# A cross-attention block on one core: VectorE scales the fourth head, ScalarE makes the second high part of K and Q ahead of that head's exponentials, x's statistics spread over four places

## The reference

```python
h = _layernorm(x, gamma, beta)                       # x: (8, 256, 256)
Q = (h @ Wq).reshape(B, NQ, 16, 64)                  # Wq: (256, 1024)
K = (context @ Wk).reshape(B, NC, 16, 64)            # context: (8, 256, 192)
V = (context @ Wv).reshape(B, NC, 16, 64)
attn = jnp.einsum('bihd,bjhd->bhij', Q, K)
attn = jax.nn.softmax(attn, axis=-1) * 64 ** -0.5
vals = jnp.einsum('bhij,bjhd->bihd', attn, V).reshape(B, NQ, 1024)
return x + vals @ Wo + bo
```

## Time and profile before

| | |
|---|---|
| time, median of 3 runs | 335.07 us (335.03 to 335.29) |
| the profiled execution's own time | 335.13 us |
| its span in the profile | 333.3 us |
| TensorE (PE) busy | 323.3 us, 97% |
| ScalarE (ACT) busy | 254.8 us, 76% |
| VectorE (DVE) busy | 234.6 us, 70% |
| GpSimd (POOL) busy | 178.3 us, 53% |

### The profile page before, as it was taken

How to read it: one execution, slowest core, us unless ns; L and a number is a source line. 1 busy time by engine, 2 the same in 40 slices (tenths; PEclk the granted TensorE clock), 3 DMA queues, 4 the chain that set the end, 5 groups by cost and what they waited for, 6 DMA issues and landing times.

```text
span 333.3 us, 9654 instructions
## 1 busy us (share of the span) xinstructions
PE 323.3 (97%) x3773; PEld 284.3 (85%) x3773; DVE 234.6 (70%) x523; ACT 254.8 (76%) x799; POOL 178.3 (53%) x332
## 2 busy tenths in 40 slices
PE   5999999999999999999999999999999999999986
PEld 4868788899888899888889988889988888998864
DVE  5888667766778677676776677776677867556754
ACT  4899897777778766888667868777777876676772
POOL 4596778437473367543673456722757336344430
PEclk9999999999999999999999999999999999999999
DMA  6960010020000200020000200002000100000000
GB/s 181 266 185 3 1 41 18 2 89 2 0 2 31 60 3 0 2 89 2 3 4 0 89 2 2 0 3 89 2 2 1 33 3 3 2 0 33 2 3 31
DMA packets 10764, 10.70 MB, mean 32 GB/s; under 512 B 960, under 2 KB 10176, under 8 KB 10720
## 3 DMA queue, kind: packets, MB, share of 16 engines
q1 hardware_dynamic: 10192, 9.64, 9.6%
q10 hardware_dynamic: 416, 0.33, 0.3%
q0 software_dynamic: 112, 0.13, 0.1%
HBM read 8.00 MB, written 2.10 MB: 30 GB/s over the span
## 4 chain that ended last, share of the span: by engine, by line
PE 86%; ACT 6%; DVE 4%; POOL 2%; DMA 1%; issue 1%; DVEq 0%; ACTq 0%
PE mix_ps L823 16%; PE o_ps L914 12%; PE ring_ps L794 12%; PE ring_ps L889 12%; PE ring_ps L968 11%; PE ring_ps L944 10%; PE ring_ps L847 9%; ACT prob L457 3%; DMA x_in<-in_x_dram 1%; PE ring_ps L867 1%; POOL prob L369 1%; PE mix_ps L760 1%; PE mix_ps L768 1%; ACT qk_hi L467 1%; DVE prob_t L737 1%
## 5 line engine op out<-in xcount | busy, mean ns | idle before, releaser
L369 POOL TENSOR_SCALAR prob<-prob,inv 128x256 f32<-128x256 f32 x256 | 120.4, 486 | 129.2 <-DVE inv L654 129.1
L457 ACT ACTIVATE prob<-ring_ps,neg_max 128x256 f32<-128x256 f32 x256 | 119.3, 481 | 21.7 <-DVE neg_max L647 21.6
L647 DVE TENSOR_REDUCE neg_max<-ring_ps 128x2 f32<-128x512 f32 x128 | 81.4, 679 | 0.8 <-PE ring_ps L794 0.8
L737 DVE COPY prob_t<-ring_ps 128x512 f32<-128x512 f32 x64 | 41.4, 686 | 37.0 <-PE ring_ps L944 37.0
L823 PE MATMUL mix_ps<-prob_t,v_sb 128*64 128x256 f32 x504 | 61.5, 385 | 0.2 <-DVE prob_t L737 0.2
L660 DVE TENSOR_TENSOR qk_lo<-ring_ps,qk_hi 128x512 fp32r<-128x512 f32 x64 | 44.2, 690 | 17.7 <-ACT qk_hi L467 17.7
L457 ACT ACTIVATION_READ_ACCUMULATOR prob<-ring_ps,neg_max 128x1 f32 x256 | 54.4, 212 | 0.0
L823 PEld LDWEIGHTS mix_ps<-prob_t,v_sb 128*64 128x64 f32 x504 | 33.4, 136 | 18.1 <-issue 0.3
L527 ACT ACTIVATE v_sb<-ring_ps 128x256 f32<-128x256 f32 x58 | 19.2, 383 | 30.1 <-PE ring_ps L968 29.6
L467 ACT ACTIVATE qk_hi<-ring_ps 128x512 fp32r<-128x512 f32 x64 | 39.6, 619 | 1.2 <-PE ring_ps L889 1.2
L944 PE MATMUL ring_ps<-ident,prob 64*128 64x64 f32 x1024 | 39.3, 226 | 0.3 <-POOL prob L369 0.3
(11 more groups left out here) (110 smaller groups left out, 638.2 us busy)
## 6 DMA issues: line engine op xcount, KB each, us to landing
x_in<-in_x_dram SPq DMA_DIRECT2D x8, 256.0 KB, 2.9
out_dram<-y_sb SPq DMA_DIRECT2D x7, 256.0 KB, 2.2
c_in<-in_ctx_dram SPq DMA_DIRECT2D x7, 192.0 KB, 2.8
w_raw<-in_L_xattn_Wq_dram SPq DMA_DIRECT2D x8, 128.0 KB, 3.1
w_raw<-in_L_xattn_Wo_dram SPq DMA_DIRECT2D x4, 256.0 KB, 4.0
w_raw<-in_L_xattn_Wk_dram SPq DMA_DIRECT2D x4, 128.0 KB, 3.7
w_raw<-in_L_xattn_Wk_dram SPq DMA_DIRECT2D x8, 64.0 KB, 3.5
w_raw<-in_L_xattn_Wv_dram SPq DMA_DIRECT2D x2, 256.0 KB, 4.7
```

The costliest lines, as they stand in the source:

```text
L369: last = nc.gpsimd.tensor_scalar(prob[:, e, r, :], prob[:, e, r, :], inv[:, e, r:r + 1], SCALE, ALU.mult, ALU.mult)
L457: last = nc.scalar.activation(prob[:, e, r, :], score_bank(u, e)[:, r * ROWS:(r + 1) * ROWS], ACT.Exp, bias=neg_max[:, e, r:r + 1], accum_ ...
L647: nc.vector.tensor_reduce(neg_max[:, e, :], score_bank(u, e)[:, :].rearrange("p (r j) -> p r j", r=RT), AX, ALU.max, negate=True).then_inc ...
L737: nc.vector.tensor_copy(turned_half(e), score_bank(u, e)[:, :] .rearrange("p (k i) -> p k i", i=HALF))\
```

## The change

VectorE multiplies head 3 by its reciprocal, right behind making it (`last_head`), and GpSimd heads 0 to 2; TensorE's second half of `turn` waits for both (`scaled_pool`, `scaled_vector`). From step 2 on ScalarE makes the second `qk_hi` before head 3's exponentials, and VectorE the second `qk_lo` before head 3's reciprocal. The statistics of sequence 2 and later are no longer taken in one piece near the end of their step: the first `bn_stats`, with the wait for the load of x, stands behind `inverse(1)`, the second behind `inverse(2)`, the aggregation behind the first `qk_lo`, the variance behind the second. The statistics of sequence 1 move to the end of step 0, and its norm from VectorE to GpSimd.

```diff
@@ gpsimd, step @@
                 if b is not None:
                     deviation(b)
-                    if b >= 2:
-                        norm(b)
+                    norm(b)
...
-                    for e in range(HEADS):
+
+                    for e in range(HEADS - 1):
                         pool.wait_ge(inv_ready, HEADS * u + e + 1)
...
-                        last.then_inc(scaled, 1)
+                        last.then_inc(scaled_pool, 1)
@@ scalar, step @@
                 if u == 2:
                     weight_hi(20)
                     weight_hi(21)
+                if u >= 2:
                     keys_hi(1)
                 probabilities(3)
-                if u != 2:
+                if u < 2:
                     keys_hi(1)
@@ vector @@
-            def statistics(b):
+            def rows_statistics(b, r):
                 k = b % 2
                 dve.wait_ge(x_loaded[k], 16 * (b // 2 + 1))
-                for r in range(RT):
-                    last = nc.vector.bn_stats(bn[:, r, :], x_in[:, k, r, :])
-                last.then_inc(stats_done, 1)
-                dve.wait_ge(stats_done, b + 1)
+                nc.vector.bn_stats(bn[:, r, :], x_in[:, k, r, :]).then_inc(stats_done, 1)
+
+            def variance(b):
+                dve.wait_ge(stats_done, RT * (b + 1))
                 nc.vector.memset(var_eps[:, :], 0.0)
...
+            def deviation_base(b):
                 dve.wait_ge(aggr_done, b + 1)
...
+            def statistics(b):
+                for r in range(RT):
+                    rows_statistics(b, r)
+                variance(b)
+                deviation_base(b)
@@ vector, step @@
+                def last_head():
+
+                    inverse(HEADS - 1)
+                    if 0 <= u < STEPS:
+                        dve.wait_ge(inv_ready, HEADS * u + HEADS)
+                        for r in range(RT):
+                            last = nc.vector.tensor_scalar(prob[:, HEADS - 1, r, :],
+                                                           prob[:, HEADS - 1, r, :],
+                                                           inv[:, HEADS - 1, r:r + 1], SCALE,
+                                                           ALU.mult, ALU.mult)
+                        last.then_inc(scaled_vector, 1)
+
...
                 inverse(1)
+
+                measured = of_seq(u, STATS, 2)
+                if measured is not None:
+                    rows_statistics(measured, 0)
...
                 inverse(2)
                 if u == -1:
                     weight_lo(4)
+                if measured is not None:
+                    rows_statistics(measured, 1)
                 keys_lo(0)
+                if measured is not None:
+                    variance(measured)
                 if u == -1:
                     weight_lo(5)
-                if u != 2:
-                    inverse(3)
+                if u < 2:
+                    last_head()
...
-                if u == 0:
-                    statistics(1)
-                if u == 1:
-                    norm(1)
                 if u == 2:
                     weight_lo(20)
                     weight_lo(21)
                 keys_lo(1)
-                if u == 2:
-                    inverse(3)
+                if measured is not None:
+                    deviation_base(measured)
+                if u >= 2:
+                    last_head()
...
-                b = of_seq(u, STATS, 2)
-                if b is not None:
-                    statistics(b)
...
                     if u == 0:
+                        statistics(1)
                         weight_lo(13)
@@ tensor, turn @@
-                    pe.wait_ge(scaled, HEADS * u + 2 * a + 2)
+                    pe.wait_ge(scaled_pool, (HEADS - 1) * u + 2 + a)
+                    if a == BATCH - 1:
+                        pe.wait_ge(scaled_vector, u + 1)
```

More of the change, by code:

```diff
@@ L191, in cross_attention_block @@
         inv_ready = sem("inv_ready")
-        scaled = sem("scaled")
+        scaled_pool = sem("scaled_pool")
+        scaled_vector = sem("scaled_vector")
         turned = sem("turned")
```

## The result

| kernel | median of six (us) | lowest to highest (us) | ratio, 95% interval |
|---|---|---|---|
| before | 335.30 | 335.03 to 335.54 | 1 |
| changed | 340.48 | 339.53 to 341.69 | 1.0157 [1.013, 1.0184] |

The change makes the kernel slower by 1.6%, 2.8 us beyond the 337.7 us of the prediction and 0.5 us over the top of its range. The six times of the changed kernel stand in two groups: three of 339.53 to 339.73 us at a mean granted clock of 0.999 to 1.000, three of 341.23 to 341.69 us at 0.995. The profiled execution is one of the first group: 339.53 us, a span of 337.7 us (before: 335.13 and 333.3).

What follows compares the result with a forecast made beforehand. TensorE, holding 86% of the chain, was taken to bound the kernel. Load 2.75, plain steps -0.72, six steps 0.42 and start 0.2 gave +2.65 on 335.13 us: 337.8, as median 337.7 us; range 336.4 to 340.0.

Steps and rivals of the forecast that it cites:

- The load: Step at 42.72: sequence 2's first bn_stats waits for x ahead of mix_lo; TensorE idles 2.75 us before output, once.
- Rival 4: x of sequence 2 has landed when VectorE reaches it: 335.1 us, 334.0 without collisions; chance 0.07.
- Second bank: In values, the earlier second qk_hi removes TensorE's wait for the second bank: 0.08 us gained per plain step.
- Start: Step 1: GpSimd also normalizes sequence 1, so its heads end later and turn(1) waits: 0.2 us lost.
- rival 3: Start or load worse, GpSimd's wo_lo going first or a slower load: 338.4 to 339.1 us; chance 0.1.
- Nothing is lost by taking the norm off VectorE: At the start, moving sequence 1's norm from VectorE to GpSimd was taken to lose nothing on VectorE's side.
- the turns in the six steps: u = 6, 10, up to 26: VectorE's scaling alternates with h_lo and x_bias; 0.15 us waiting, 0.07 us net loss each.
- Rival 1: No turns between VectorE and GpSimd in the six steps: 336.8 us, 336.6 with nothing lost at the start; chance 0.2.
- Rival 2: Steps with statistics: x_norm goes before VectorE's second scaling, TensorE loses 0.85 us in five steps: 342 us; chance 0.08.
- GpSimd's own part gets shorter and is not on the path.: Scaling of heads: GpSimd, rid of head 3, has less to do and delays nothing; no cost in the sum.
- the plain steps: Steps without transposes of x or the context: nine of them gain 0.08 us each, -0.72 us in the sum.
- That is 2.75 us of idle TensorE, once: Step at 42.72: TensorE starts output at 51.5 instead of 48.75, and no later slack gives it back.

Runs made afterwards that it cites:

- 1: Changed kernel with only sequence 2's statistics put back in one piece near the end of step 3: 337.05 us, 1.0051.
- 2: Changed kernel with GpSimd making sequence 0's bias ahead of weight split 22, so the load of x goes out earlier: 337.25 us, 1.0048.
- 9: Kernel before with only the statistics of sequences 2 and later spread over the four places: 339.87 us, 1.0115.
- 3: Changed kernel with GpSimd's h_lo held back behind VectorE's scaling in steps 6, 10, up to 26: 339.44 us, 1.0107.
- 4: Changed kernel with GpSimd's h_lo held back behind VectorE's scaling in step 2 alone: 340.49 us, 1.0148.
- 6: Changed kernel, sequence 0's bias ahead of split 22, h_lo held behind VectorE's scaling; sequence 1's norm on VectorE 334.92 us, on GpSimd 334.69 us.
- 8: Kernel before with only the norm of sequence 1 moved to GpSimd: 336.55 us, 1.0042.
- 7: Changed kernel with sequence 0's bias ahead of weight split 22 but still waiting for that weight's high part: 338.40 us, 1.0098.
- experiment 10: Kernel before plus ScalarE's move and head 3 on VectorE, no spread or norm move: 338.53 us; then with sequence 1's statistics later: 337.97 us.

## Why the prediction was wrong

In short: the order of things and the largest cost came as forecast, but two costs were too small or missing in the sum, and a third, the clock, was not in it at all. The first group, 339.53 to 339.73 us, still lies within the range; the clock took the other three executions, and with them the median, out of it.

**Right.** *The load*: 2.75 us forecast, 2.66 in step 3, and the sum's largest term by far; shown by taking the wait away from both sides (1, 2) and by making it alone (9). The 2.66 belong to a load that was read 2.56 us after its issue; in the profiles of 3, 4 and 9 it was 2.76 to 2.84 us, and `output` began 0.2 to 0.3 us later. Rival 4 is out: the load goes out at 48.74, VectorE wants it near 47.8. (Its 335.1 us should be 335.0 by its own terms.) *Second bank*: nine steps at -0.06 instead of -0.08. *Start*: +0.28 against +0.2, but that the sizes meet is partly luck: it is not one loss at the end of `turn(1)`, but 0.51 lost in step 1 and 0.23 won in step 0, which the prediction did not see. VectorE's split of weight 13 went ahead of `wo_lo` by only 0.07 us (22.79 and 22.86), so rival 3's start did not come. *"Nothing is lost by taking the norm off VectorE"* held beside VectorE's head 3: putting the norm back cost 0.27 in step 1 (6). Without the change's other parts the same move lost 1.0 us there (8).

**Mis-sized: the turns in the six steps.** 0.07 us each was forecast, 0.18 measured, 0.66 us in all. The order of the turns came as drawn: VectorE's scalings behind `h_lo` and the first `x_bias`, ending 9.23 us into the step (84.23 + 1.33 - 76.33), by the prediction 9.20 (200.25 - 191.05). What was too small is the 0.05 us left for the signal: in the trace `turn`'s second half begins at 85.71, 0.15 after the scaling's end at 85.56. `turn` lost 0.26 instead of 0.15, and the second bank won 0.08 as forecast (1.27 for 1.35). Rival 1 is out. Rival 2 is out too: the scaling's median over all steps is 353 ns, and no `turn` waits in the steps with `rstd` and `x_norm`.

**The step that failed.** "GpSimd's own part gets shorter and is not on the path." That was weighed for the six steps that have `h_lo` at the place of the scaling, and not for step 2, the first that has `h_lo` and the only one of these in which VectorE splits value weights, with TensorE waiting for the second half. There GpSimd's earlier `h_lo` came between the halves: a term that the sum had at nothing, +0.55 us (4). The Trainium skill, page "SBUF — State Buffer", section "SBUF: two separate sides", which the prediction used for the six steps, has GpSimd and a VectorE instruction with two SBUF inputs exclude each other for a whole instruction, whoever starts first. `wv_lo` reads two SBUF tensors, and the trace agrees there as well: 1.28 us for the pair alone, 1.83 with `h_lo` between.

With these two the forecast would have been 337.7 + 0.66 + 0.55 = 338.9 us; the later first `scores` (0.25), the plain steps (0.18), the start (0.08) and the load (-0.09) bring it to 339.3, some 0.3 below the first group.

**Left out of the sum: the clock.** "That is 2.75 us of idle TensorE, once" prices the idle at its length. In three of six executions the time was 1.8 us longer, at a mean granted clock of 0.995. None of these three was profiled. Three profiles with the same wait (3, 4, 9) show the granted clock at 0.50 from 0.3 to 1.1 us after TensorE's new start, and 5.23 to 5.31 us from the first product of `output` to the next `scores` instead of 3.76: about 1.5 us for the clock, and 0.2 to 0.3 for the later load. That it is the idle in step 3 is shown by 1, 2 and 6, where without it none of 32 executions (5, 5 and 22) fell below clock 0.999, and by 7, where the idle was 1.42 us; that it comes with the late load and none of the other edits, by 9. The Trainium skill, page "TensorE: Matmul & The Clock Gate", section "What's actually happening", says that an idle engine's clock is halved and that the window over which activity is watched runs freely and does not start with the kernel; by that the same idle could cost the clock in one execution and not in the next, and the drops 0.3, 0.6 and 1.1 us behind the idle agree. Its table asks for a longer idle before the clock is halved than any here; there the measurement decides. What picks the executions is not shown: in the profiles the idle was 2.39 us where the clock held, and 2.73, 2.66 and 2.64 us where it fell (3, 4, 9), so the load's landing may decide as well as the window.

**Where the change's own gain went.** ScalarE's move alone gives 0.9963 [0.995, 0.9976] and is the best kernel of these. VectorE's share of the scaling wins nothing on top: with every collision removed it ends at 0.9987, and its profile is 0.3 us longer than that of ScalarE's move alone, nearly all of it in steps 0 and 1. It frees GpSimd, which nothing waits for in a plain step, and in return asks for the statistics' move, the norm's move and a hold on `h_lo`.

## What to carry to other kernels

Before a wait is moved forward in an engine's queue, look for its latest release in the whole run, not in a typical step: here five sequences find their load long there, and one, the first that reuses a buffer, does not. Work taken off an idle engine makes its next work start sooner, and if that work and an engine on the path hold each other up, as they do here, every step in which the two can now meet has to be checked. An idle TensorE costs its length, and may cost clock as well: here 2.4 to 2.7 us of it took about another 1.5 us in two executions of three.

## What was not expected of the hardware

- The clock fell behind an idle of TensorE of only 2.6 to 2.7 us, with the engine busy again for 0.3 to 1.1 us, and cost about 1.5 us.
- In step 0 of experiment 10 `var_eps`, 128x2 elements, took 0.74 us beside GpSimd's weight split, before 0.19: a tiny VectorE instruction stood as long as a large one of GpSimd.
- At a granted clock of 1.00 throughout, the twelve products of `output` take 1.36 us in most steps and 1.42 us in some steps of some kernels (0.118 us from product to product instead of 0.113). In experiment 10's first profile six steps have it, some 0.35 us in all. What sets the pace stays open.
